# A banded attention and expert-routing kernel: the values become the held operand, in four 32-column strips, and the transposed probabilities stream past them

## The chip, the cores and the metric

The kernel runs on one core of a Trainium2 chip. The metric is device time in microseconds (us); three runs of the kernel before gave 1156.02 us as their median. Six engines matter: TensorE (PE in the profile, with its weight loads shown as PEld), VectorE (DVE), ScalarE (ACT), GpSimd (POOL), SyncE (SP) and the DMA queues. Each engine works through its own instructions in program order, and they meet at semaphores.

A matrix product here is always "held operand" against "streamed operand": the held one (128 partitions by up to 128 columns) is loaded into the array, the streamed one passes through it, and each held column becomes one partition of the result in PSUM.

## The reference

Eight sequences of 1024 tokens, 128 features, float32. The block is layer norm, windowed attention, residual, layer norm, a mixture of experts, residual:

```
q, k, v = split_heads(xn @ Wq), split_heads(xn @ Wk), split_heads(xn @ Wv)   # 16 heads of 8
scores  = einsum('bhld,bhlwd->bhlw', q, k_win) * scale      # each token sees the last 64 keys
attn    = softmax(scores)
ctx     = einsum('bhlw,bhlwd->bhld', attn, v_win)
x       = x + ctx @ Wo
...
expert_weights, top_experts = top_k(softmax(xf @ w_router), 2)   # 8 experts, capacity 2048 slots each
h = gelu(einsum('ech,ehf->ecf', xb, w1)); y = einsum('ecf,efh->ech', h, w2)
x = x + (gated y, added back to its tokens) + bias
```

## The kernel before

**Tiles and stages.** The 8192 tokens are 64 tiles of 128, worked in 32 pairs. The first stage (to about 800 us of the trace) does the attention of all pairs and, once per sequence of four pairs, the routing. The second stage (from about 846 us) runs the experts over gathered slots. The change touches the first stage.

**One pair.** A pair `n` has two tiles (`s` = 0, 1), each tile two blocks of 64 queries, each block 16 heads. The heads are worked in 8 slots per pair (`k` = 0 to 7): slot k belongs to tile k // 4, block (k // 2) % 2 and half of the heads k % 2, and holds four products `c` of two heads each. A row block of one product is 2 heads x 64 queries = 128, its columns are 128 keys, of which a window mask in `kT` leaves 64 per query.

**One slot on TensorE** (function `pair` of the tensor block, L1066):

- `probs_T(n, k)`, L1002: four transposes of the probabilities of this slot into the one PSUM bank `pt_ps`;
- `score(.., k + LEAD)`, L993: four score products, three slots ahead, into one of four banks;
- `weighted(.., k - 1)`, L1015: four products of the slot before. The held operand is the transposed probabilities (128 columns), the streamed one is the values of two heads and a column of ones (17 columns). The results lie as query rows in `o_ps[s]`, one bank per tile; the 17th column is the softmax's denominator;
- in some slots one of the small steps: `prep_T`, `query_key`, `values` for the next pair (L968 to L979), `context_T` (L1021) and `project` (L1029) of a finished tile, `router_T` and `router` (L1036, L1041).

Every float32 product is carried out as two instructions, each with its own weight load, so that four products stand as x8 in the trace; a transpose is one instruction.

**The other engines in a slot.** VectorE: `score_max` (L661) takes the row maximum of the scores, `probs_T` (L666) copies the transposed probabilities to SBUF in six of eight slots, layer-norm steps (L618 to L652) lie between; `normalise` (L673, L677) divides a finished tile's sums, `residual` (L685) adds the projected tile to `x_sb`. ScalarE: `exps` (L509, four activations, 128x128 each) three slots ahead, `probs_T` (L515) in slots 0 and 5, and copies for the small steps (L467 to L525). GpSimd: `spread_queries` (L360) builds the block-diagonal queries, and in the pair behind a routed one it issues the indirect DMAs that send rows to their slots (L370).

**What sets the order.** It is written out by hand: each engine has a function `pair` with the eight slots. A finished tile goes weighted -> normalise -> context_T (TensorE) -> context_T (ScalarE) -> project -> residual. TensorE waits before the first `weighted` of a tile until the residual of the last tile in that bank is done (`s_x2`), before `weighted` and before the next `probs_T` until the copy of the transposed probabilities is done (`s_pt_sb`).

Of the kernel before, what the change touches and what calls it, by code (L numbers as in the profile page):

```python
# [30 lines left out]
VW = 2 * DH + 2  # L31
# [16 lines left out]
def moe_block_kernel(nc, x, wq, wk, wv, wo, w_router, w1, w2, bias, out):  # L48
    ctx = ExitStack()
    with ctx:  # L50
# [51 lines left out]
        probs = sb("probs", [P, 4, 4, P])  # L102
        probsT = sb("probsT", [P, 2, 4, P])
        rden = sb("rden", [P, 2, 2 * HP])
        ctx_sb = sb("ctx_sb", [P, 2, 3 * HP, DH])
# [21 lines left out]
        w1_hl = sb("w1_hl", [P, 2, 2, F], F32R)  # L127
        xT_hl = sb("xT_hl", [P, 2, 2, 4 * P], F32R)
# [11 lines left out]
        o_ps = bank[5:7]  # L140
# [6 lines left out]
        def ctx_view(s):  # L147
            return o_ps[s][:, 0:2 * HP * VW].rearrange("p (j c) -> p j c", c=VW)

# [25 lines left out]
        s_pv = sem("s_pv")  # L175
        s_ctx = sem("s_ctx")
# [271 lines left out]
        def _(act):  # L448
# [67 lines left out]

            def context_T(n, s):
# [13 lines left out]
            def pair(n, g=None, first=False):  # L531
                for k in range(UNITS):
# [32 lines left out]
            walk(act, pair)  # L565
            context_T(NPAIR - 1, 1)
# [24 lines left out]
        def _(dve):  # L591
# [77 lines left out]
            def normalise(chain, n, s):  # L669

                dve.wait_ge(s_pv, UNITS * n + 4 * s + 4)
# [136 lines left out]
            for i, free in enumerate((s_x2, s_xn2T, s_lg_sb, s_pt_sb, s_rows, s_out, s_sent, f_added)):  # L808
                nc.vector.memset(scratch[:, i:i + 1], 0.0).then_inc(free, START)
# [40 lines left out]
            def pair(n, g=None, first=False):  # L850
                chain = Chain(n * PER + PRE + ROUTE_STEPS * pair.routed + (1 if first else 0))
                for k in range(UNITS):
# [14 lines left out]
                    if k == 0 and not first:  # L867
                        normalise(chain, n - 1, 1)
# [55 lines left out]
            def gated(ee, q, c):  # L924
# [6 lines left out]
                else:  # L931
# [3 lines left out]
                                        in0=o_ps[c % 2][:, :].rearrange("p (k d) -> p k d", k=4),  # L935
# [26 lines left out]
        def _(pe):  # L962
# [42 lines left out]
            def weighted(n, k):  # L1005
# [60 lines left out]
            def pair(n, g=None, first=False):  # L1066
                for k in range(UNITS):
# [5 lines left out]
                    if k > 0:  # L1073
                        weighted(n, k - 1)
                    elif not first:
                        weighted(n - 1, UNITS - 1)
# [3 lines left out]
                    if k == 1:  # L1080
                        if not first:
                            context_T(n - 1, 1)
                        query_key(n + 1)
                    if k == 2 and not first:
                        project(n - 1, 1)
                    if k == 3:
# [110 lines left out]
```

## Time and profile before

| | us |
|---|---|
| median of three runs | 1156.02 |
| lowest, highest | 1154.77, 1157.13 |
| span of the profiled execution | 1155.7 |
| TensorE busy, its weight loads busy | 990.6 (86%), 942.3 (82%) |
| VectorE busy | 644.9 (56%) |
| ScalarE busy | 609.6 (53%) |
| GpSimd busy | 488.5 (42%) |

The page gives the profiled execution by its span, 1155.7 us, which lies 0.3 us from the median of the runs; nothing else of that execution is timed. The span has to be read by stage. Until about 800 us it is a train of pairs, most of them 21.53 us long; in the expert stage other limits hold. Within a pair, the chain of waits and the order in time say which engine is the bound. A matmul's recorded duration includes the way through the array; what one costs in a row of many is the distance between the starts, so a group "x8" of length 0.89 us in the chain is eight at 0.112 us.

### The profile page before, as it was taken

The numbers are of one execution on the slowest core, as the hardware profiler recorded it, in microseconds if no ns is written. First come the engines' busy times: TensorE is split into PE (matmuls) and PEld (weight loads), VectorE is DVE, ScalarE is ACT, GpSimd is POOL, SyncE is SP. The second block draws the span as 40 slices with busy tenths as digits, with TensorE's granted clock in tenths as the row PEclk, the third lists the DMA queues.
The fourth block names the chain that finished last, engine by engine and source line by source line (L and its number), as shares of the span: only waits on it lengthen the run. The fifth ranks groups of instructions, "written<-read, shape, count | busy, mean of one in ns | idle before, by whom it ended". The sixth has DMA issues, their size and how long they took to land.

```text
span 1155.7 us, 24887 instructions
## 1 busy us (share of the span) xinstructions
PE 990.6 (86%) x7670; PEld 942.3 (82%) x7670; DVE 644.9 (56%) x1980; ACT 609.6 (53%) x1898; POOL 488.5 (42%) x445
## 2 busy tenths in 40 slices
PE   2999998899899889989997998999605998889791
PEld 1899998799799889988997997999604997878691
DVE  5777787488468747856774786578521121212110
ACT  2777676466467647655673765567202442434330
POOL 4122124421712352162135225212531877777777
PEclk9999999799799979988997998899656999889896
DMA  8900001100100110010011001000122455455533
GB/s 186 390 17 18 11 10 47 32 18 18 56 12 9 41 37 9 18 60 17 9 36 42 9 18 56 22 9 31 50 65 87 54 90 90 76 84 89 89 33 34
DMA packets 61821, 60.14 MB, mean 52 GB/s; under 512 B 6721, under 2 KB 50648, under 8 KB 60736
## 3 DMA queue, kind: packets, MB, share of 16 engines
q1 hardware_dynamic: 34944, 40.18, 10.6%
q0 software_dynamic: 22528, 17.22, 10.3%
q10 hardware_dynamic: 4288, 2.10, 1.2%
q8 instruction: 18, 0.29, 0.1%
q14 instruction: 43, 0.35, 0.1%
HBM read 17.70 MB, written 31.59 MB: 43 GB/s over the span
## 4 chain that ended last, share of the span: by engine, by line
PE 44%; issue 18%; POOL 11%; DVE 11%; another core or an unknown queue 6%; ACT 4%; DMA 3%; ACTq 1%; DVEq 1%; POOLq 0%; SPq 0%
PE bank L993 15%; PE bank L1015 11%; POOL out L429 11%; PE bank L1002 8%; PE bank L1029 2%; DMA out<-y_sb,xg 2%; ACT probs L509 2%; ACT kT L479 2%; DVE negmax L661 2%; DVE probsT L666 1%; PE bank L979 1%; PE bank L1021 1%; DVE xn L652 1%; PE bank L973 1%
## 5 line engine op out<-in xcount | busy, mean ns | idle before, releaser
L509 ACT ACTIVATE probs<-bank,negmax 128x128 f32<-128x128 f32 x1036 | 295.2, 368 | 285.2 <-DVE negmax L661 278.4
L360 POOL TENSOR_TENSOR qbd<-qT,quadmask 128x512 f32<-128x512 f32 x132 | 134.5, 1040 | 522.8 <-ACT qT L467 400.3
L993 PE MATMUL bank<-kT,qbd 128*128 (+1 forms) x2072 | 295.1, 289 | 0.0
L993 PEld LDWEIGHTS bank<-kT,qbd 128*128 128x128 f32 x2072 | 273.2, 206 | 0.0
L1015 PEld LDWEIGHTS bank<-v_sb,probsT 128*128 128x128 f32 x2048 | 263.1, 200 | 3.7 <-issue 3.4
L1015 PE MATMUL bank<-v_sb,probsT 128*128 (+1 forms) x2048 | 258.9, 259 | 3.7 <-issue 3.5
L429 POOL DMA_INDIRECT out<-y_sb,xg x128 | 198.2, 1548 | 81.0 <-DVE y_sb L934 42.0
L661 DVE TENSOR_REDUCE negmax<-bank 128x4 f32<-128x512 f32 x259 | 177.9, 687 | 75.5 <-PE bank L993 42.4
L1002 PE MATMUL bank<-ident,probs 128*128 128x128 f32 x1024 | 170.1, 291 | 39.2 <-ACT probsT L515 26.6
L666 DVE COPY probsT<-bank 128x512 f32<-128x512 f32 x192 | 132.5, 690 | 122.7 <-PE bank L1002 76.0
L1002 PEld LDWEIGHTS bank<-ident,probs 128*128 128x128 f32 x1024 | 125.0, 152 | 56.5 <-ACT probsT L515 30.6
L581 ACT ACTIVATE hT<-bank 128x512 f32<-128x512 f32 x128 | 76.5, 597 | 144.2 <-PE bank L1137 136.4
L370 POOL DMA_INDIRECT slots_dram<-send_rows,slot_id x112 | 109.1, 974 | 32.1 <-issue 32.1
L1147 PE MATMUL bank<-w_sb,hT 128*128 128x128 f32 x1024 | 121.9, 278 | 0.0
L1137 PE MATMUL bank<-xT_hl,w_hl 128*128 128x512 f32 x384 | 105.1, 426 | 17.9 <-DVE xT_hl L921 17.9
L1147 PEld LDWEIGHTS bank<-w_sb,hT 128*128 128x128 f32 x1024 | 119.5, 195 | 0.1
L1137 PEld LDWEIGHTS bank<-xT_hl,w_hl 128*128 128x128 f32 x384 | 75.6, 204 | 34.8 <-issue 11.1
L934 DVE TENSOR_TENSOR y_sb<-bank,xg 128x512 f32<-128x512 f32 x32 | 22.1, 691 | 124.9 <-DMA out<-y_sb,xg 67.3
L921 DVE TENSOR_TENSOR xT_hl<-bank,xT_hl 128x512 fp32r<-128x512 f32 x32 | 22.1, 690 | 113.6 <-ACT xT_hl L574 102.8
L479 ACT COPY kT<-bank 32x256 f32 (+1 forms) x264 | 83.2, 361 | 2.4
L1124 PE MATMUL bank<-ident,xg 128*128 128x128 f32 x128 | 21.0, 290 | 34.5 <-DMA xg<-slots_dram 34.5
L1124 PEld LDWEIGHTS bank<-ident,xg 128*128 128x128 f32 x128 | 17.1, 151 | 39.6 <-issue 31.0
(114 smaller groups left out, 930.6 us busy)
## 6 DMA issues: line engine op xcount, KB each, us to landing
slots_dram<-empty_rows SPq DMA_DIRECT2D x8, 1096.0 KB, 15.4
xg<-slots_dram SPq DMA_DIRECT2D x32, 274.0 KB, 4.3
rows_sb<-xn SPq DMA_DIRECT2D x33, 128.0 KB
out<-xbias SPq DMA_DIRECT2D x32, 128.0 KB
w_sb<-in_L_ffn_w SPq DMA_DIRECT2D x16, 256.0 KB
send_rows<-rows_sb SPq DMA_DIRECT2D x7, 548.0 KB, 3.0
out<-y_sb,xg POOLq DMA_INDIRECT x128
slots_dram<-send_rows,slot_id POOLq DMA_INDIRECT x112
```

What stands on the lines that cost most here:

```text
L360: last = pool.tensor_tensor(out=qbd[s][half][:, :, :, :], in0=q.unsqueeze(2).to_broadcast([P, 2, HQ, BLK]), in1=heads.to_broadcast([P, 2, ...
L370: pool.indirect_dma_start(out=slots_dram, out_offset=bass.IndirectOffsetOnAxis(ap=slot_id[:, k, j:j + 1].bitcast(U32), axis=0), in_=rows[: ...
L429: pool.indirect_dma_start(out=out, out_offset=bass.IndirectOffsetOnAxis(ap=xg[:, r, 4 * c + k, ROW - 1:ROW].bitcast(U32), axis=0), in_=y_s ...
L479: last = nc.scalar.copy(windows.rearrange("p (t w) j -> p t w j", t=2), blocks[:, :, odd, :].unsqueeze(2).to_broadcast([32, 2, 2, BLK]))
L509: last = nc.scalar.activation(probs[:, k % 4, c, :], scores[k % 4][:, c * P:(c + 1) * P], ACT.Exp, bias=negmax[:, k % 4, c:c + 1])
L661: nc.vector.tensor_reduce(negmax[:, k % 4, :], scores[k % 4][:, :].rearrange("p (c j) -> p c j", c=4), AX.X, ALU.max, negate=True).then_in ...
L666: nc.vector.tensor_copy(probsT[:, k % 2, :, :].rearrange("p c j -> p (c j)"), pt_ps[:, :]).then_inc(s_pt_sb, 1)
L993: last = mm(scores[k % 4][:, c * P:(c + 1) * P], qbd[s][half][:, blk, h:h + 2, :].rearrange("p h q -> p (h q)"), keys.rearrange("p o j -> ...
L1002: last = nc.tensor.transpose(pt_ps[:, c * P:(c + 1) * P], probs[:, k % 4, c, :], ident[:, :])
L1015: last = mm(ctx_view(s)[:, blk * HP + j, 0:2 * DH + 1], probsT[:, k % 2, c, :], v, start=True, stop=True)
L1137: last = mm(bank[f][:, :], w1_hl[:, r, a, f * P:(f + 1) * P], xT_hl[:, c % 2, b, :], start=(i == 0), stop=(i == 2))
L1147: last = mm(o_ps[c % 2][:, k * D:(k + 1) * D], hT[:, c % 2, f, k * P:(k + 1) * P], w2_sb[:, r, f, :], start=(f == 0), stop=(f == FC - 1))
```

## The change

It turns the weighted sums round. The values of two heads, with their ones column, become the held operand: `VW` grows from 18 to 32, so that a product's values fill a strip of 32 columns, and the four products of a slot use the four strips of the array, with their results in partitions 0-31, 32-63, 64-95 and 96-127 of one new bank `u_ps`. The transposed probabilities, 128 columns, stream. The sums of a tile then lie transposed (values by queries). For every tile ScalarE copies the whole bank to SBUF (`weighted_out`, a new 128x512 copy), and TensorE transposes it back by four transposes (`weighted_T`) into `o_ps`, where `normalise` finds it as before, at a distance of 32 instead of 18.

There is one bank `u_ps` and one bank `o_ps` now for both tiles. The first `weighted` of a tile waits until `weighted_out` of the tile before has run (`s_u_sb`); `weighted_T` waits for that copy and for the residual of the tile before (`s_x2`); `normalise` waits for `weighted_T` (`s_uT`). The steps of the second tile move by one slot: `normalise` on VectorE from slot 0 to 1, `context_T` from slot 1 to 2 on TensorE and ScalarE, `project` from slot 2 to 3. TensorE's loop is written out over the four pairs of a sequence. `probs` gets another place in SBUF, and the expert stage addresses the same two banks by other names.

```diff
-VW = 2 * DH + 2
+VW = 32
...
-        o_ps = bank[5:7]
+        u_ps = bank[5]
+        o_ps = [bank[6], bank[6]]
...
+            def weighted_out(n, s):
+                act.wait_ge(s_pv, UNITS * n + 4 * s + 4)
+                nc.scalar.copy(u_sb[:, s, :, :].rearrange("p i q -> p (i q)"), u_ps[:, :]).then_inc(s_u_sb, 1)
...
-                    if k == 1 and not first:
+                    if k == 0:
+                        if not first:
+                            weighted_out(n - 1, 1)
+                        prep_T(n + 1)
+                    if k == 2 and not first:
                         context_T(n - 1, 1)
-                    if k == 0:
-                        prep_T(n + 1)
+                    if k == 4:
+                        weighted_out(n, 0)
...
-                dve.wait_ge(s_pv, UNITS * n + 4 * s + 4)
+                dve.wait_ge(s_uT, 2 * n + s + 1)
...
-                    if k == 0 and not first:
+                    if k == 1 and not first:
                         normalise(chain, n - 1, 1)
...
                 if k % 4 == 0:
-                    pe.wait_ge(s_x2, START + 2 * n - 1 + s)
+                    pe.wait_ge(s_u_sb, START + 2 * n + s)
                 for c in range(4):
-                    j = 4 * half + c
-                    v = v_sb[:, bass.ds(n % 2, 1), 2 * s + blk, j, 0:2 * DH + 1].rearrange("p o c -> p (o c)")
-                    last = mm(ctx_view(s)[:, blk * HP + j, 0:2 * DH + 1], probsT[:, k % 2, c, :], v, start=True, stop=True)
+                    v = v_sb[:, p % 2, 2 * s + blk, 4 * half + c, :]
+                    last = mm(u_ps[32 * c:32 * c + 32, (k % 4) * P:(k % 4 + 1) * P], v, probsT[:, k % 2, c, :],
+                              start=True, stop=True)
                 last.then_inc(s_pv, 1)
+
+            def weighted_T(n, s):
+                pe.wait_ge(s_u_sb, START + 2 * n + s + 1)
+                pe.wait_ge(s_x2, START + 2 * n + s)
+                for i in range(4):
+                    last = nc.tensor.transpose(o_ps[s][:, i * P:(i + 1) * P], u_sb[:, s, i, :], ident[:, :])
+                last.then_inc(s_uT, 1)
```

On TensorE, in slots 5 and 6 of a pair, this stands before (L1002 is `probs_T`, L993 `score`, L1015 `weighted` of the slot before, L1036 `router_T`, L1021 `context_T`):

```order
L1002 MATMUL bank<-ident,probs 128x128 [waits s_pt_sb,s_exp]
L1002 MATMUL bank<-ident,probs 128x128 x3
L993 MATMUL bank<-kT,qbd 128x128 [waits s_k_sb,s_qbd]
L993 MATMUL bank<-kT,qbd 128x128 x3
L1015 MATMUL bank<-v_sb,probsT 128x17 [waits s_x2,s_pt_sb]
L1015 MATMUL bank<-v_sb,probsT 128x17 x3
L1036 MATMUL bank<-ident,xn 128x128 [waits s_xn2,s_v_sb]
```

and in the same place this stands now (L1016 `probs_T`, L1007 `score`, L1029 `weighted`, L1037 `weighted_T`, L1058 `router_T`):

```order
L1016 MATMUL bank<-ident,probs 128x128 [waits s_pt_sb,s_exp]
L1016 MATMUL bank<-ident,probs 128x128 x3
L1007 MATMUL bank<-kT,qbd 128x128 [waits s_k_sb,s_qbd]
L1007 MATMUL bank<-kT,qbd 128x128 x3
L1029 MATMUL bank<-probsT,v_sb 32x128 [waits s_u_sb,s_pt_sb]
L1029 MATMUL bank<-probsT,v_sb 32x128 x3
L1037 MATMUL bank<-ident,u_sb 128x128 [waits s_x2,s_u_sb]
L1037 MATMUL bank<-ident,u_sb 128x128 x3
L1058 MATMUL bank<-ident,xn 128x128 [waits s_xn2,s_v_sb]
```

The first product of the tile's second half of slots now waits for ScalarE's copy instead of for a residual, and four transposes follow it.

On ScalarE, slots 4 to 6 of a pair stand so before (L509 `exps`, L515 the copy of the transposed probabilities, L525 `router_T`):

```order
L509 ACTIVATE probs<-bank,negmax 128x128 x4
L515 COPY probsT<-bank 128x512
L507 ISA
L509 ACTIVATE probs<-bank,negmax 128x128 x4
L524 REGISTER_ALU
L525 ACTIVATE xn2T<-bank 128x256
```

and so now (L514 `exps`, L524 `weighted_out`, L520 the copy of the transposed probabilities, L534 `router_T`):

```order
L514 ACTIVATE probs<-bank,negmax 128x128 x4
L524 COPY u_sb<-bank 128x512
L520 COPY probsT<-bank 128x512
L512 ISA
L514 ACTIVATE probs<-bank,negmax 128x128 x4
L533 REGISTER_ALU
L534 ACTIVATE xn2T<-bank 128x256
```

The new copy stands behind the slot's four exponentials and ahead of the copy that TensorE's next transposes wait for.

## Rows read from the trace of the kernel before

**Rows 1.** Page: busy time of each engine, and TensorE's granted clock in 40 slices.

```profile
PE 990.6 (86%) x7670; PEld 942.3 (82%) x7670; DVE 644.9 (56%) x1980; ACT 609.6 (53%) x1898; POOL 488.5 (42%) x445
...
PEclk9999999799799979988997998899656999889896
```

**Rows 2.** Busy time by stretch: three whole pairs of 21.53 us apart, a routed pair, two behind it.

```profile
core 0: us, PE busy (x) PEld busy (x) DVE busy (x) ACT busy (x) POOL busy (x), PEclk, DMA share, GB/s
240.80:262.33 21.53, 21.53 (x189) 21.08 (x188) 16.28 (x49) 15.61 (x55) 4.76 (x5) 1.00 0.04 12
...
571.93:595.15 23.22, 22.36 (x199) 21.51 (x199) 21.38 (x76) 15.87 (x54) 4.76 (x5) 1.00 0.04 12
595.15:627.70 32.55, 27.15 (x190) 26.09 (x190) 15.96 (x48) 14.39 (x49) 20.33 (x21) 0.84 0.18 60
627.70:652.85 25.15, 23.49 (x189) 22.66 (x190) 17.08 (x53) 16.99 (x58) 4.76 (x5) 0.93 0.04 11
```

**Rows 3.** Chain of waits over one pair (240.8 to 262.4): start, length, what.

```profile
241.48 0.89 PE bank L993 x8
242.37 0.80 PE bank L1015 x8
...
256.86 0.44 PE bank L1002 x4
```

**Rows 4.** TensorE in time, 246.2 to 251.0: start, length; across a 64-row group.

```profile
247.86 0.96 PE L1015 MATMUL bank<-v_sb,probsT 128*128 x8
248.76 0.71 PE L1029 MATMUL bank<-wo_sb,ctxT 64*128 64x128 f32 x4
249.40 0.66 PE L1002 MATMUL bank<-ident,probs 128*128 128x128 f32 x4
249.89 1.06 PE L993 MATMUL bank<-kT,qbd 128*128 x8
```

**Rows 5.** TensorE in time, 252.0 to 259.2: slots 4 and 5.

```profile
252.12 0.60 PE L1002 MATMUL bank<-ident,probs 128*128 128x128 f32 x4
...
253.45 0.96 PE L1015 MATMUL bank<-v_sb,probsT 128*128 x8
...
254.74 1.06 PE L993 MATMUL bank<-kT,qbd 128*128 x8
255.63 0.96 PE L1015 MATMUL bank<-v_sb,probsT 128*128 x8
```

**Rows 6.** VectorE in the same stretch.

```profile
252.81 0.68 DVE L666 COPY probsT<-bank 128x512 f32<-128x512 f32 x1
253.41 0.86 DVE L618 BATCH_NORM_STATS2 stats<-x_sb 128x6 f32 x4
254.19 0.68 DVE L661 TENSOR_REDUCE negmax<-bank 128x4 f32<-128x512 f32 x1
```

**Rows 7.** ScalarE in the same stretch.

```profile
254.90 1.14 ACT L509 ACTIVATE probs<-bank,negmax 128x128 f32<-128x128 f32 x4 [0.81 <-DVE negmax L661]
255.91 0.60 ACT L515 COPY probsT<-bank 128x512 f32<-128x512 f32 x1
```

**Rows 8.** ScalarE, then TensorE, in slots 0 and 1 (240.8 to 245).

```profile
243.13 1.14 ACT L509 ACTIVATE probs<-bank,negmax 128x128 f32<-128x128 f32 x4 [1.03 <-DVE negmax L661]
244.15 0.39 ACT L486 COPY xnT<-bank 128x256 f32<-128x256 f32 x1
...
244.60 0.63 PE L1015 MATMUL bank<-v_sb,probsT 128*128 x5
```

**Rows 9.** Longest waits of 595 to 653, the two pairs behind a routed one.

```profile
ACT probs L509 <- DVE negmax L661: 25.7, 13, 7.6
...
DVE probsT L666 <- remote: 7.1, 2, 4.1
```

**Rows 10.** Page: GpSimd's issues to the slots (busy, mean ns).

```profile
L370 POOL DMA_INDIRECT slots_dram<-send_rows,slot_id x112 | 109.1, 974 | 32.1 <-issue 32.1
```

More of the change, by code:

```diff
@@ L127, in moe_block_kernel @@
         w1_hl = sb("w1_hl", [P, 2, 2, F], F32R)
+        with nc.sbuf_tensor("probs", [P, 4, 4, P], F32) as probs:
+            pass
         xT_hl = sb("xT_hl", [P, 2, 2, 4 * P], F32R)
@@ L565, in _ @@
             walk(act, pair)
+            weighted_out(NPAIR - 1, 1)
             context_T(NPAIR - 1, 1)
@@ L806, in _ @@
             nc.vector.memset(kT[96:128, 3, 0, :], 0.0)
-            for i, free in enumerate((s_x2, s_xn2T, s_lg_sb, s_pt_sb, s_rows, s_out, s_sent, f_added)):
+            for i, free in enumerate((s_x2, s_xn2T, s_lg_sb, s_pt_sb, s_u_sb, s_rows, s_out, s_sent, f_added)):
                 nc.vector.memset(scratch[:, i:i + 1], 0.0).then_inc(free, START)
@@ L1003, in probs_T, with weighted @@
                 last.then_inc(s_pt, 1)
-            def weighted(n, k):
+            def weighted(n, p, k):
                 s, blk, half = k // 4, (k // 2) % 2, k % 2
@@ L1064, in counts, with pair @@
                 last.then_inc(s_pos, 1)
-            def pair(n, g=None, first=False):
+            def pair(n, p, g=None, first=False):
                 for k in range(UNITS):
@@ L1073, in pair @@
                     if k > 0:
-                        weighted(n, k - 1)
+                        weighted(n, p, k - 1)
                     elif not first:
-                        weighted(n - 1, UNITS - 1)
+                        weighted(n - 1, p + 1, UNITS - 1)
                     if k == 0:
@@ L1081, in pair @@
                         if not first:
-                            context_T(n - 1, 1)
+                            weighted_T(n - 1, 1)
                         query_key(n + 1)
                     if k == 2 and not first:
-                        project(n - 1, 1)
+                        context_T(n - 1, 1)
                     if k == 3:
+                        if not first:
+                            project(n - 1, 1)
                         values(n + 1)
                     if k == 5:
+                        weighted_T(n, 0)
                         pe.wait_ge(s_v_sb, n + 2)
@@ L1098, in pair @@
                         project(n, 0)
-            pair(0, first=True)
+            pair(0, 0, first=True)
             pe.wait_ge(c_pool, 21)
-            walk(pe, pair)
-            weighted(NPAIR - 1, UNITS - 1)
+            for p in range(1, PAIRS_PER_SEQ):
+                pair(p, p)
+            with pe.Fori(1, BATCH) as b:
+                for p in range(PAIRS_PER_SEQ):
+                    pair(b * PAIRS_PER_SEQ + p, p, b - 1 if p == ROUTED_AT else None)
+            weighted(NPAIR - 1, PAIRS_PER_SEQ - 1, UNITS - 1)
+            weighted_T(NPAIR - 1, 1)
             context_T(NPAIR - 1, 1)
@@ L1146, in results @@
                     for f in range(FC):
-                        last = mm(o_ps[c % 2][:, k * D:(k + 1) * D], hT[:, c % 2, f, k * P:(k + 1) * P],
+                        last = mm(bank[5 + c % 2][:, k * D:(k + 1) * D], hT[:, c % 2, f, k * P:(k + 1) * P],
                                   w2_sb[:, r, f, :], start=(f == 0), stop=(f == FC - 1))
```

8 lines of the change are left out of this document (5 added, 3 removed).

## The prediction, made before the changed kernel had run

> **What bounds the kernel now.** I read the page first [rows 1]: TensorE is busy for 86% of the span, no other engine for more than 56%, and its clock, in tenths, stands at 9 in most slices with dips to 7. That is a mean over stages, so I cut the stretch of pairs into its pairs. The common pair takes 21.53 us, and TensorE is busy in all 21.53 of it, at full clock, with VectorE at 16.28, ScalarE at 15.61 and GpSimd at 4.76 [rows 2]. The routed pair takes 23.22 (TensorE 22.36, VectorE 21.38). The pair behind it takes 32.55, with 5.4 us in which TensorE is idle and a clock of 0.84; the one after that 25.15. There ScalarE waits for VectorE's maxima, VectorE waits for something that the profile calls remote [rows 9], and GpSimd is busy for 20.33 us with its issues at 0.97 us each [rows 2, 10]. So four pairs take 102.4 us, and 25 of 32 pairs go at TensorE's pace or nearly so; seven do not. The expert stage is untouched.
>
> Then the chain of waits over a common pair: it never leaves TensorE. Eight score instructions take 0.89 us, 0.112 each; the weighted sums go at the same pitch (0.80, and the rest stands in the next piece); four transposes take 0.44, 0.109 each [rows 3]. The weighted sums stream 17 columns and the scores 128, yet both need 0.112 us an instruction. The sums thus pay for loading 128 held columns, and the scores for streaming 128, or for both.
>
> **The products turned round.** 8 slots of 8 instructions a pair, 0.89 us each slot. The held operand shrinks to 32 columns, the streamed one grows from 17 to 128, so one instruction alone still costs about 0.112 us: nothing is won but by strips that run side by side. The trace has no strips, so I bound a slot's products. Above: one instruction after the other, 8 x 0.112 = 0.89 us. Below: all four strips at once and only the two instructions of one product behind each other, 2 x 0.112 = 0.22. In every row instructions start in program order, and the two of one product stand next to each other and use the same strip. The second must wait for the first, and the next product's first can start only behind that second. So the eight overlap only at the three joints between products: 5 x 0.112 = 0.56 us. I take that, which is worked out from the scores' pitch, and keep both ends for the range.
>
> **Changing the shape of the array.** `project` is the one group now that uses the array in another shape, 64*128. From the start of the weighted group ahead of it to the next score group are 249.89 - 247.86 = 2.03 us [rows 4]; where nothing stands between, 254.74 - 253.45 = 1.29 [rows 5]. The difference of 0.74 is 4 x 0.112 = 0.45 for its instructions and 0.29 for going into the shape and out again. I take 0.30 for both, 0.15 for one. Every slot would now go in and out: 8 x 0.30 a pair. The bounds are nothing (only a cut by rows pays) and 0.30. `project` stands right behind the strips in slots 3 and 7, so that one of its own changes goes: -0.15 x 2.
> The Trainium skill says in "TensorEngine Tiling (Array Packing)", Key Properties, that a change of tiling mode, and not only of the tile, drains the engine. The trace shows it for 64 rows; no row shows it for 32 columns. By that rule the price of 0.30 would hold for the strips too, and it speaks against this change.
>
> So a slot's group costs 0.56 + 0.30 = 0.86 against 0.89: -0.03, or -0.3 us a pair. TensorE's main gain is eaten by the shape changes.
>
> **The way back.** Eight transposes a pair at 0.109: +0.9 us, all on TensorE, which has no gap. Sum on TensorE: -0.3 - 0.3 + 0.9 = +0.3.
>
> **The new copy.** ScalarE gets two 128x512 copies a pair, 0.60 each [rows 7]: 15.6 + 1.2 = 16.8 of 21.5, which fits. But TensorE now waits for them, since there is one bank `u_ps`. In slot 5 the first sums of tile 1 need `weighted_out` of tile 0. What is queued ahead of that copy on ScalarE is four exponentials, which need VectorE's maximum of scores that TensorE made in slot 4. Before, the four transposes of slot 4 end at 252.72; VectorE copies (252.81), takes the layer norm's statistics (253.41, 0.86), the maximum (254.19) [rows 5, 6]; the exponentials start at 254.90, and the next copy at 255.91 lasts until 256.51 [rows 7]. The new copy takes that place. With 0.1 for the signal, the sums can load at 256.6; now they load 0.11 before their start at 255.63, at 255.52 [rows 5]. Stall: 1.1 us. What was next on ScalarE, the copy of the transposed probabilities, comes 0.6 later, at 257.1, while TensorE's transposes that need it stand behind the late sums (0.86) and the four new transposes (0.44): covered. In slot 0 the exponentials end at 244.15 (the next copy's start), the new copy at 244.75, so the sums can load at 244.85 in place of 244.49 [rows 8]: 0.35 us. Below, these stalls could be nothing if ScalarE ran further ahead; it does not, it waited 0.81 and 1.03 us for the maxima there. If TensorE became faster per slot by some amount, each stall would grow by that amount: the path over VectorE and ScalarE does not shrink. VectorE's division now waits for the way back, but its result is needed one slot later and it has over 5 us a pair to spare. Sum of stalls: 1.45.
>
> **The sum.** A pair at TensorE's pace: +0.3 + 1.45 = +1.75 us; 25 of them, +44. In the seven long pairs 5.4 us of idle TensorE hide the transposes; the copy (0.6 each) stands in their chain through ScalarE: I take +0.7, with 0 and 1.75 as bounds, so +5. At the end of the stage one copy and four transposes lengthen the last tile: +1, and the longer fill of ones in `v_sb` at the start under +1. 1155.7 (the span) + 44 + 5 + 2 = 1207. The span is 0.3 us below the median of the runs, so that I name 1207 for the run as well. Its own range is 1190 to 1225.
>
> **The rivals.**
> *Strips one after another* (22%). A slot's products take 0.89 + 0.30: +0.30 x 8 = +2.4, with -0.3 and +0.9; the stalls shrink to 0.8, since TensorE comes later itself. +3.8 x 25 = +95, the long pairs +10, the ends +2: 1263. For it: two float32 instructions with 32-column loads between, and no row shows two matmuls side by side. Against it: held weights and PSUM partitions are disjoint.
> *Strips overlap fully, or the shape change is free* (22%). With all four at once, 0.22 + 0.30 a slot: -0.37 x 8 = -3.0, -0.3 and +0.9 make -2.4, but the stalls grow by 0.34 each to 2.1: -0.3 x 25 = -7, +5 + 2: 1156. With no price for the shape but 0.56 for the products: -0.33 x 8 + 0.9 = -1.7, stalls 2.05: +0.35 x 25 = +9, +7: 1171. So even the gain that was worked out comes back as a wait for ScalarE. Together 1148 to 1176.
> The Trainium skill, "TensorE: Matmul & The Clock Gate", Measured speedup vs the span model, has packed products start about 4 ns apart and three column strips at 2.38 times the speed. That would put the four strips at the lower bound here, if the two instructions of a product did not stand between; no run here shows it yet.
> *Both* (10%): 0.22 us a slot, no shape price. -0.67 x 8 + 0.9 = -4.5; stalls 1.45 + 2 x 0.64 = 2.7; -1.8 x 25 = -45 + 7: 1118. ScalarE, with 16.8 us of work and waits of 0.8 to 1 us in several slots, would then be the bound, so 1118 to 1140.
> *The clock falls* (8%). TensorE has no idle time in a common pair now and a clock of 1.00; where it is idle for 5.4 of 32.55 us, the mean clock is 0.84 [rows 2]. With 1.45 us of stall and the shape changes in 23 us it could spend part of each pair at the lower of its two levels, 1.2 in place of 2.4 GHz. At a mean clock of 0.93, as in the pair of 25.15, some 7% of the pair is added to the forecast: 25 x 1.6 = +40: 1247. It decides once it touches the common pairs, not only the ones behind the routed one. Against it: the pair of 23.22 has 0.9 us of idle TensorE and still 1.00.
>
> **How the numbers follow.** Forecast 38%, strips in turn 22%, full overlap or free shape 22%, both 10%, clock 8%. Cases of both signs exist, but those on the slower side hold most of the chance. The range 1142 to 1268 holds the forecast, the clock case, the middle cases and somewhat over half of the strips in turn, which itself is uncertain by 15 us either way: about 82%. About 0.2% (2.3 us) is what a measurement of this kernel can tell from no change. Faster: the 10% of both and 9 of the 22% around 1156 and 1171, 20% in all with rounding; within 0.2%: 5%; slower: 75%.
>
> **What the profile of the changed kernel would show.** The chain of a common pair: still TensorE, now broken twice by ScalarE's copy `u_sb` and VectorE's maximum. TensorE in time: from the last score start to the next group's first start about 0.97 us if I am right, near 1.3 if the strips go in turn, near 0.64 if they overlap fully. Waits: TensorE's `weighted` line on ScalarE's `u_sb` copy, about 1.1 us and 0.35 us, once each a pair. A common pair of 23.3 us. The forecast is wrong if a common pair is under 22 or over 24.5 us, if no gap stands at the strips' edges, or if that wait is missing.

## The result: 1.5% slower, and the profile after

| | before | after |
|---|---|---|
| median of the runs, us | 1156.31 | 1174.04 |
| span of the profiled execution, us | 1155.7 | 1171.7 |
| stage of pairs (second pair's preparation to the last's) | 768.8 | 783.0 |

The ratio is 1.015, with a 95% interval of 1.0136 to 1.0165: 17.7 us slower. 1207 was forecast with a range of 1142 to 1268. The sign holds and the time lies in the range, but the loss is 17.7 us where 51 were forecast, a third. On a second chip, both kernels again gave 1157.8 and 1182.2 us (below), a ratio of 1.021.

First the page: busy time of each engine [rows 1].

```profile
PE 907.6 (77%) x7926; PEld 772.3 (66%) x7926; DVE 666.4 (57%) x1981; ACT 641.4 (55%) x1962; POOL 489.2 (42%) x445
```

TensorE has lost 83 us of busy time (990.6 before) and the kernel is slower. Then busy time by stretch [rows 2]: an early common pair, a later one, a routed one, the two behind it.

```profile
core 0: us, PE busy (x) PEld busy (x) DVE busy (x) ACT busy (x) POOL busy (x), PEclk, DMA share, GB/s
96.80:118.75 21.95, 19.72 (x200) 16.58 (x196) 16.71 (x50) 16.62 (x55) 4.82 (x5) 1.00 0.05 13
351.04:373.46 22.42, 19.75 (x200) 16.55 (x197) 17.39 (x50) 16.62 (x55) 4.76 (x5) 1.00 0.05 13
373.46:396.43 22.97, 20.14 (x209) 16.85 (x206) 20.47 (x74) 16.88 (x56) 4.76 (x5) 1.00 0.04 12
396.43:432.00 35.57, 22.74 (x196) 18.93 (x196) 18.95 (x50) 16.76 (x55) 20.40 (x21) 0.82 0.17 57
432.00:455.05 23.05, 20.13 (x201) 16.93 (x197) 17.74 (x51) 16.51 (x55) 4.76 (x5) 0.98 0.05 14
```

A common pair, 21.53 us before, is 21.95 early and 22.42 later, and TensorE now idles for some 2.7 us of it. The routed pair went from 23.2 to 23.0. The two behind it: before 57.7 together, now 58.6. Summed over the stage: the first six pairs +2.8, seven routed ones -1.9, six later common ones +5.3, the twelve behind routed ones +7.9 (the six with the sends +10.6, the six after them -2.6); the start -1.3 and what follows the last pair +3.1. That is the 16.0 us between the spans.

TensorE in time, slots 3 to 5 of the common pair (start, length) [rows 5]:

```profile
358.48 0.43 PE L1029 MATMUL bank<-probsT,v_sb 128*32 128x128 f32 x8
359.43 0.71 PE L1051 MATMUL bank<-wo_sb,ctxT 64*128 64x128 f32 x4 [0.53 <-ACT ctxT L528]
360.73 0.71 PE L993 MATMUL bank<-wv_sb,xnT 128*128 128x128 f32 x4 [0.59 <-ACT kT L484]
...
361.72 1.06 PE L1007 MATMUL bank<-kT,qbd 128*128 128x128 f32 x8
362.70 0.42 PE L1029 MATMUL bank<-probsT,v_sb 128*32 128x128 f32 x8
363.06 0.66 PE L1016 MATMUL bank<-ident,probs 128*128 128x128 f32 x4
363.55 1.06 PE L1007 MATMUL bank<-kT,qbd 128*128 128x128 f32 x8
365.69 0.42 PE L1029 MATMUL bank<-probsT,v_sb 128*32 128x128 f32 x8 [1.08 <-ACT u_sb L524]
366.04 0.66 PE L1037 MATMUL bank<-ident,u_sb 128*128 128x128 f32 x4
```

and the same slot 4 before [rows 5]:

```profile
252.56 1.06 PE L993 MATMUL bank<-kT,qbd 128*128 x8
253.45 0.96 PE L1015 MATMUL bank<-v_sb,probsT 128*128 x8
254.26 0.63 PE L1002 MATMUL bank<-ident,probs 128*128 128x128 f32 x4
254.74 1.06 PE L993 MATMUL bank<-kT,qbd 128*128 x8
```

The strips' eight instructions last 0.42 us with their way through the array, against 0.96. From score group to score group, slot 4 takes 363.55 - 361.72 = 1.83 us where it took 254.74 - 252.56 = 2.18. Three times in these rows TensorE waits for ScalarE: for the copied context (0.53), the keys (0.59) and the copied sums (1.08). ScalarE in the same stretch [rows 7]:

```profile
359.00 0.38 ACT L528 ACTIVATE ctxT<-bank 64x256 f32<-64x256 f32 x1
359.40 1.28 ACT L484 COPY kT<-bank 32x256 f32 x4
...
364.01 1.14 ACT L514 ACTIVATE probs<-bank,negmax 128x128 f32<-128x128 f32 x4 [0.93 <-DVE negmax L675]
365.03 0.60 ACT L524 COPY u_sb<-bank 128x512 f32<-128x512 f32 x1
365.50 0.62 ACT L520 COPY probsT<-bank 128x512 f32<-128x512 f32 x1
```

The chain of waits over that place shows the path of the prediction: maximum, exponentials, copy, sums.

```profile
363.39 0.60 DVE negmax L675
...
364.28 0.88 ACT probs L514 x3
365.16 0.48 ACT u_sb L524
365.64 0.04 issue
365.69 0.42 PE bank L1029 x8
```

Slot 1 has the same wait, shorter:

```profile
353.29 0.42 PE L1029 MATMUL bank<-probsT,v_sb 128*32 128x128 f32 x8 [0.47 <-ACT u_sb L524]
```

The figure in brackets is idle time of the array alone. Measured from start to start, less the 0.20 us that stands at an edge of the strips anyway, the waits of the common pair are 0.54 (slot 1), 0.60 for the context and 0.66 for the keys (slot 3), and 1.15 us (slot 5): 2.95 in all.

### The profile page after: what moved, and what is told of

Read it like the earlier page. It is cut to its first block, busy times and chain, and to the rows that moved or that the text cites. A ratio compares the mean times of both kernels' runs of the same rounds, so it can differ in the third digit from the quotient of the medians.

```text
span 1171.7 us, 24626 instructions
## 1 busy us (share of the span) xinstructions
PE 907.6 (77%) x7926; PEld 772.3 (66%) x7926; DVE 666.4 (57%) x1981; ACT 641.4 (55%) x1962; POOL 489.2 (42%) x445
## 3 DMA queue, kind: packets, MB, share of 16 engines
q8 instruction: 76, 1.25, 0.4%
## 4 chain that ended last, share of the span: by engine, by line
PE 29%; issue 21%; DVE 15%; ACT 13%; POOL 11%; another core or an unknown queue 5%; DMA 3%; ACTq 1%; DVEq 1%; POOLq 0%; SPq 0%
POOL out L434 10%; PE bank L1007 7%; ACT probs L514 7%; PE bank L1016 6%; DVE negmax L675 5%; PE bank L1029 4%; PE bank L1037 4%; ACT kT L484 3%; ACT u_sb L524 3%; DMA out<-y_sb,xg 2%; DVE stats L632 2%; PE bank L993 2%; PE bank L1051 1%; PE bank L987 1%
## 5 line engine op out<-in xcount | busy, mean ns | idle before, releaser
L514 ACT ACTIVATE probs<-bank,negmax 128x128 f32<-128x128 f32 x1036 | 296.6, 371 | 241.0 <-DVE negmax L675 228.3
L1007 PE MATMUL bank<-kT,qbd 128*128 128x128 f32 x2072 | 285.2, 283 | 0.0
L1007 PEld LDWEIGHTS bank<-kT,qbd 128*128 128x128 f32 x2072 | 264.1, 200 | 0.0
L1016 PE MATMUL bank<-ident,probs 128*128 128x128 f32 x1024 | 166.1, 287 | 22.4 <-DVE probsT L680 14.2
L1029 PE MATMUL bank<-probsT,v_sb 128*32 128x128 f32 x2048 | 113.2, 294 | 90.1 <-ACT u_sb L524 82.3
L1016 PEld LDWEIGHTS bank<-ident,probs 128*128 128x128 f32 x1024 | 124.7, 149 | 38.0 <-DVE probsT L680 17.1
L1029 PEld LDWEIGHTS bank<-probsT,v_sb 128*32 128x32 f32 x2048 | 42.2, 110 | 125.5 <-ACT u_sb L524 64.1
L1177 PE MATMUL bank<-w_sb,hT 128*128 128x128 f32 x1024 | 119.4, 275 | 0.0
L1177 PEld LDWEIGHTS bank<-w_sb,hT 128*128 128x128 f32 x1024 | 116.9, 192 | 0.1
L1051 PE MATMUL bank<-wo_sb,ctxT 64*128 64x128 f32 x256 | 45.9, 300 | 18.7 <-ACT ctxT L528 12.4
L1051 PEld LDWEIGHTS bank<-wo_sb,ctxT 64*128 64x128 f32 x256 | 33.5, 188 | 34.0 <-ACT ctxT L528 21.0
```

The lines of the kernel that those rows point to most:

```text
L514: last = nc.scalar.activation(probs[:, k % 4, c, :], scores[k % 4][:, c * P:(c + 1) * P], ACT.Exp, bias=negmax[:, k % 4, c:c + 1])
L1007: last = mm(scores[k % 4][:, c * P:(c + 1) * P], qbd[s][half][:, blk, h:h + 2, :].rearrange("p h q -> p (h q)"), keys.rearrange("p o j -> ...
L1016: last = nc.tensor.transpose(pt_ps[:, c * P:(c + 1) * P], probs[:, k % 4, c, :], ident[:, :])
L1029: last = mm(u_ps[32 * c:32 * c + 32, (k % 4) * P:(k % 4 + 1) * P], v, probsT[:, k % 2, c, :], start=True, stop=True)
L1177: last = mm(bank[5 + c % 2][:, k * D:(k + 1) * D], hT[:, c % 2, f, k * P:(k + 1) * P], w2_sb[:, r, f, :], start=(f == 0), stop=(f == FC - 1))
```

## The experiments

Two explanations stand against each other. Theory W: the strips give their full gain, and waits for ScalarE take it back. Rival P: shape changes and transposes eat the gain. Unless said otherwise an edit is made to the changed kernel; ratios are to the kernel before, run beside it.

### 1. Where ScalarE's copy stands, and the shared bank

First, on ScalarE, `weighted_out` ahead of the exponentials (its two calls behind them go):

```diff
                     if k in BY_ACT:
                         probs_T(n, k)
+                    if k == 0 and not first:
+                        weighted_out(n - 1, 1)
+                    if k == 4:
+                        weighted_out(n, 0)
                     if k + LEAD < UNITS:
                         exps(n, k + LEAD)
...
-                            weighted_out(n - 1, 1)
...
-                    if k == 4:
-                        weighted_out(n, 0)
```

> The changed kernel, but on ScalarE the copy of the sums stands ahead of the slot's four exponentials in slots 0 and 4 instead of behind them. Theory W (the strips pay in full, and waits for ScalarE's copy give it back): in the changed kernel's common pair TensorE's sums wait 0.5 us in slot 1 and 1.15 us in slot 5 for that copy; ahead of the exponentials it falls into ScalarE's wait for the maximum, so both waits go: -1.6 us in some 25 pairs, about 1134 us. Rival P (TensorE's changes of shape and the eight transposes eat the gain, and VectorE and ScalarE would set the pace anyway): the waits only move, 1165 to 1176 us.

1156.5 us, ratio 0.998 (0.997 to 1.000): between the two cases. Both waits for the copy are gone from the common pair, which takes 21.29 us: 1.13 less, not 1.6, since the router's logits now wait some 0.25 us and three smaller gaps of 0.08 us open; the slot-3 waits stay as they were. The six pairs with sends grew from 209 to 224 us, while the six after them fell by 15.

Then a bank of its own for each tile; `weighted_T` no longer waits for a residual, since `weighted` does:

```diff
-        u_ps = bank[5]
-        o_ps = [bank[6], bank[6]]
+        u_ps = o_ps = bank[5:7]
...
-                    pe.wait_ge(s_u_sb, START + 2 * n + s)
+                    pe.wait_ge(s_x2, START + 2 * n - 1 + s)
...
-                pe.wait_ge(s_x2, START + 2 * n + s)
```

> The changed kernel, but each tile's sums have a bank of their own and are transposed back into the same bank; the order on ScalarE stays. The sums of the next tile no longer wait for the copy, only the transposes behind them do. Theory W: of the 0.5 and 1.15 us of wait a pair 0.4 each is covered by the sums themselves: -1.0 us in 25 pairs, about 1148 us. Rival P: no change beyond 5 us, 1168 to 1176 us.

1152.5 us, 0.996 (0.994 to 0.997), nearer theory W. Common pair 21.60; of the waits for the copy, 0.78 us before `weighted_T` in slot 5 and 0.1 in slot 1 are left.

Both edits together:

> Both edits: the copy ahead of the exponentials, and a bank of its own for each tile. Theory W: the two take away the same waits, so hardly more than the copy's place alone: 1128 to 1136 us. Rival P: 1165 to 1176 us. If the remaining wait for ScalarE in slot 3 (0.5 us for context, 0.8 us for the keys) grows in their place, 1145 to 1155 us.

1143.5 us, 0.987 (0.986 to 0.989). That is in none of the three cases and nearest the last, but not for its reason: the slot-3 waits are 0.60 and 0.66 us, as before, and have not grown. The common pair is 21.29 as with the copy first alone; the gain over it lies in the pairs with sends (206 us for six in place of 224). Rival P falls: TensorE's instructions and their order are the same in these three, only what they wait for and where they write differs, and 17.6, 21.5 and 30.5 us of the 1174.0 came off.

### 2. What the strips do

One strip for all four products of a slot:

```diff
-                    last = mm(u_ps[32 * c:32 * c + 32, (k % 4) * P:(k % 4 + 1) * P], v, probsT[:, k % 2, c, :],
+                    last = mm(u_ps[0:32, (k % 4) * P:(k % 4 + 1) * P], v, probsT[:, k % 2, c, :],
```

> The changed kernel, but the four products of a slot all use the first strip of 32 columns and write the same 32 partitions, so that three of four heads' sums are lost (the other partitions of the bank hold ones). Shape changes, copy and transposes stay. Theory W: the eight instructions go one after another at 0.112 us, 0.89 us in place of 0.24: +5.2 us a pair on TensorE, of which the waits for ScalarE's copy give back up to 2: +3.2 to +4 us in 25 pairs, 1250 to 1275 us. If strips gave nothing, 1174 us.

1257.8 us, 1.086 (1.084 to 1.089), as theory W had it. The common pair is 25.06, 2.64 more. Read from the single records of the trace, the eight starts stand 0.109 us apart (the first two 0.133), 0.79 us in all, where four strips have them within 0.154: four starts 7 ns apart, and from 0.133 on four more.

```profile
386.15 1.06 PE L1008 MATMUL bank<-kT,qbd 128*128 128x128 f32 x8
387.13 1.06 PE L1030 MATMUL bank<-probsT,v_sb 128*32 128x128 f32 x8
388.13 0.66 PE L1038 MATMUL bank<-ident,u_sb 128*128 128x128 f32 x4
```

Two strips, products 0 and 1 on the first and 2 and 3 on the second:

```diff
-                    last = mm(u_ps[32 * c:32 * c + 32, (k % 4) * P:(k % 4 + 1) * P], v, probsT[:, k % 2, c, :],
+                    last = mm(u_ps[32 * (c // 2):32 * (c // 2) + 32, (k % 4) * P:(k % 4 + 1) * P], v, probsT[:, k % 2, c, :],
```

> The changed kernel, but products 0 and 1 of a slot use the first strip of 32 columns and products 2 and 3 the second, so half of the heads' sums are lost (the rest of the bank holds ones). It tells how four strips come to take two pitches and not the five of the prediction. From the first to the last recorded start of the eight instructions four strips took 0.15 us and one strip 0.79. Theory F (starts strictly in order, the two halves of a product next to each other, as the prediction had it): 6 pitches between, 0.65 us, about 1235 us. Theory I (in order, but the first halves of all four products stand before the second halves): 4 pitches between, 0.44 us, about 1205 us. Theory Q (each strip runs its own instructions, whatever stands between them): 3 pitches between, 0.33 us, about 1193 us.

The starts stand at 0, 13, 133, 146, 242, 255, 351 and 365 ns, within 4 ns in 220 of 256 groups: three pitches, theory Q. The records do not name the strip of a start, but the other two theories would need four and six pitches. So two strips run side by side although the kernel's order puts the first strip's four instructions ahead of the second's. The common pair is 23.25 us, between 22.42 and 25.06.

This kernel and e10 (below) ran where the kernel before took 1075.5 us, so their totals (1143.7 and 1120.3) compare only with that: 1.063 and 1.041. The waits that the profile calls remote, 67 us on VectorE in the first trace, are missing from both traces, and GpSimd issues its DMAs as before (0.97 us each); why is open. A later kernel on the same chip had them again.

### 3. Side edits, and the price of a shape alone

The kernel before with the change's side edits alone: TensorE's loop written out, `VW = 32` and the new place of `probs`.

> The kernel before with the change's side edits alone: TensorE's loop written out over four pairs, values at a distance of 32, probs at its new place; sums as before. Theory W: none of these is on the way of a pair that TensorE keeps busy: common pair 21.53 us, within 3 us of the kernel before. Rival S (the longer instruction stream or the new places cost part of the 17.7 us): 1160 us or more.

1158.0 us, 1.001 (1.000 to 1.002), common pair 21.53. Theory W.

The kernel before with its projection over all 128 rows:

```diff
-        wo_sb = sb("wo_sb", [HP * DH, 2, D])
+        wo_sb = sb("wo_sb", [P, 2, D])
...
-        ctxT = sb("ctxT", [HP * DH, 2, 2, 2, BLK])
+        ctxT = sb("ctxT", [P, 2, 2, 2, BLK])
```

> The kernel before, but the projection uses all 128 rows of the array (rows 64 to 127 of its weights are zero), so that the only group with another shape has the common one. It tells the price of a shape change by itself. Theory W: 0.30 us for going in and out, twice a pair: common pair 20.93 us, -15 us in 25 pairs, about 1141 us. Rival (the 0.29 us that was read lies in something else, the wait for the copied context or ScalarE's copy): within 3 us of the kernel before.

1154.1 us, 0.997 (0.996 to 0.998). The total is 2.6 us less, the rival's case, but its reason does not hold: the common pair lost 0.31 us of the 0.60. In the trace the stretch from the sums' start over the projection to the next score start is 0.25 us shorter (1.78 where it was 2.03 [rows 4]), but TensorE then waits 0.16 us for the keys in slot 3. So the price of going in and out is real, 0.25 rather than 0.30, and ScalarE's keys are near the bound already in the kernel before. Less arrives in the total because the twelve pairs behind routed ones took 2.9 us more than in the first trace; why is open.

### 4. The wait in slot 3

The context transposes of the second tile (TensorE) and their copy (ScalarE, shown) at the end of slot 1 instead of in slot 2:

```diff
                     if k == 1:
                         query_key(n + 1)
                         keys(n + 1, (0, 1))
+                        if not first:
+                            context_T(n - 1, 1)
...
-                    if k == 2 and not first:
-                        context_T(n - 1, 1)
```

> The changed kernel with one edit alone: the second tile's context transposes and their copy at the end of slot 1 instead of in slot 2. In the changed kernel's common pair TensorE waits 0.60 us for the copied context and 0.66 us for the keys in slot 3, which the prediction did not have. Theory W: half or more of these 1.26 us goes, 0.5 to 1.0 us in 25 pairs, 1149 to 1162 us. Rival: the two waits for the copied sums grow by as much, 1171 to 1176 us.

It ran beside the kernel before at 1075.5 us (above), so it was run again, with both kernels and the best version so far:

> The kernel before, unchanged, traced where the next three run. In the last two experiments it took 1075.5 us in place of 1156 and VectorE's waits that the profile calls remote (67 us in the first trace) were missing from the traces of both. If this chip is like the first ones: 1154 to 1158 us, common pair 21.53, the pair with the sends near 32.6. If it is like the last: about 1075 us, common pair again 21.53, the pair with the sends near 25.

> The changed kernel, unchanged. On a chip like the first: ratio 1.0136 to 1.0165 as before. On a chip like the last: the common pair costs the same +0.88 us, but the long pairs are no longer held by the sends and the change's cost shows there too, so 1120 to 1130 us, a ratio of 1.04 to 1.05.

> The changed kernel with the context early alone, beside the changed kernel itself on one chip. Theory W: the wait of slot 3 shrinks, common pair 22.17 against 22.42 us, 4 to 12 us less than the changed kernel. Rival: the same time within 2 us.

1157.8 us before, 1182.2 changed (1.021, 1.0195 to 1.0229), 1181.6 with the context early (1.020). The common pair fell from 22.42 to 22.16: the wait for the context (0.60) went, the keys' (0.68) stayed, 0.27 came in front of the context. The early pairs rose from 21.96 to 22.41. The rival holds by its time, though not by its reason: the waits for the copied sums did not grow (1.08 us of idle time in slot 5 before the edit, 1.07 with it). The six later common pairs gave 1.6 us, the early ones took 0.8 of it back, and the routed ones stayed as they were. The common pair of the changed kernel repeats to 0.01 us on both chips; the six pairs with sends do not (209 and 226 us). The stretch of one of them in the second trace of the changed kernel, then waits in it (total, times, longest):

```profile
291.74:330.32 38.58, 23.50 (x197) 19.52 (x197) 18.55 (x52) 16.75 (x55) 20.29 (x21) 0.80 0.16 53
```

```profile
PE bank L1029 <- ACT u_sb L524: 6.8, 2, 5.9
...
DVE probsT L680 <- remote: 5.5, 1, 5.5
...
PE bank L1051 <- ACT ctxT L528: 4.5, 2, 4.1
DVE negmax L675 <- remote: 4.3, 1, 4.3
```

While GpSimd sends, single VectorE instructions start 4 to 6 us late for something that the profile calls remote, and the wait for ScalarE's copy, 1.15 us in a common pair, becomes 5.9. That the sends are behind these waits is shown further down: without them VectorE has no remote wait in the whole trace.

On top of e3, the context early:

> The changed kernel with the copy first and own banks, and besides the second tile's context transposes and their copy stand at the end of slot 1 instead of in slot 2. In the common pair of the kernel without this (21.29 us) TensorE waits in slot 3, 0.5 us for the copied context and 0.6 us for the keys, with ScalarE idle from 344.14 to 344.72 just ahead. Theory W: 0.4 to 0.8 us less in 25 pairs, 1124 to 1134 us. Rival D (VectorE's maxima behind the layer norm steps set the pace in slots 1 to 5): the wait moves to slot 4, within 4 us of 1143.5.

1139.1 us, 0.983 (0.982 to 0.985), common pair 21.05: 0.24 less. The 4.4 us lie between the two cases. With the projection over all rows:

> The kernel with the copy first, own banks and the context early, with the projection over all 128 rows too. The projection follows the strips, so one shape change of two goes: 0.15 us twice a pair. Theory W, if TensorE is still the pace in those slots: 4 to 8 us less than with the context early alone. Rival D: no more than 2 us less.

1136.9 us, 0.982 (0.980 to 0.984): 2.3 us less, again between the cases, and by the totals not told from the one before; the common pair fell to 20.92. Repeated beside the kernel before of the second chip:

> The best version so far (copy first, own banks, context early, full rows), unchanged. On a chip like the first 1134 to 1139 us, ratio 0.982. On a chip like the last its common pair is 20.92 against 21.53 as there; 1065 to 1090 us, and whether it still beats the kernel before depends on its long pairs.

1134.0 us, 0.980 (0.978 to 0.981).

Then the keys, ahead of the exponentials in slot 2:

```diff
+                    if k == 2:
+                        keys(n + 1, (2, 3))
                     if k + LEAD < UNITS:
                         exps(n, k + LEAD)
...
-                    if k == 2:
-                        keys(n + 1, (2, 3))
```

> The best version so far (copy first, own banks, context early, full rows) with one more edit: in slot 2 ScalarE copies the second half of the keys ahead of the four exponentials. In its common pair of 20.92 us TensorE's value products wait 0.68 us for these keys. Theory W: that wait goes, 0.4 to 0.7 us in 25 pairs, 1116 to 1128 us. Rival D (the exponentials, 0.6 us later, are then late for VectorE and TensorE): within 3 us of the best version or slower, 1131 to 1140 us.

**1118.3 us, 0.967 (0.965 to 0.968): the best version, 39 us faster than the kernel before beside it.** Common pair 20.04. The wait for the keys, which the prediction did not have, is gone, and 0.9 us a pair with it: in the trace without this edit it was 0.76 us from start to start, and some 0.16 less now stand before the router's logits. A stretch of 20.20 us among the common pairs, in which TensorE is idle for 0.20:

```profile
335.10:355.30 20.20, 20.00 (x200) 16.51 (x199) 18.04 (x58) 16.60 (x56) 4.77 (x5) 1.00 0.05 14
```

### 5. The sends, and a long branch

The kernel before without the DMAs that send rows to their slots:

```diff
-                        pool.indirect_dma_start(
...
+                        pool.sem_inc(s_scat, 16)
```

> The kernel before without GpSimd's 128 indirect DMAs that send rows to their slots (the semaphore is counted up instead; the experts then work on empty slots). It takes the cause out of the long pairs. Theory L (the sends alone make the pair behind a routed one 32.6 us and the one after it 25.1): both fall to near 21.5 us, and the stage of pairs to about 690 us. If another cause holds them long: above 25 us.

1046.0 us. The pair with the sends falls from 32.6 to 21.53, exactly a common one; the one after it is 23.5. The stage of pairs takes 693.4 us, and VectorE has no remote wait left (67 us in the first trace). Theory L holds for the kernel before, except for 2 us in the pair after. Another 36 us went behind the pairs, where the experts work on empty slots.

The changed kernel without them:

> The changed kernel without the sends, beside the one before without them. Theory L: without sends every pair is common or routed, and the change costs what the common pairs cost: 7 x (-0.27) and 24 x 0.5 to 0.9, +12 to +20 us in the stage of pairs, with the long pairs' further +9 to +16 us gone. Rival: the long pairs keep a share of the loss without the sends, over +25 us.

1081.6 us, so 35.6 more, and the rival holds: the pair behind a routed one keeps some 27.0 us. Six such pairs hold 32 of the 36 us. Near the end of one:

```profile
207.34 0.71 PE L1047 MATMUL bank<-wo_sb,ctxT 64*128 64x128 f32 x4
211.06 0.65 PE L1012 MATMUL bank<-ident,probs 128*128 128x128 f32 x4 [3.02 <-issue]
```

TensorE idles for 3 us for nothing that the profile shows. Then its granted clock falls to the lower level, 1.2 GHz, for 3.4 us from 212.3 on; behind the later five branches it does so for 6.8 us each. In the trace its branch back to the loop's start lasts 3.3 to 4.2 us in every kernel with strips and four pairs written out, and 0.21 in the kernel before and in e5, whose loop is written out too. The pages' instruction queue (packets, MB, share):

```profile
q8 instruction: 22, 0.36, 0.1%
```

for e5, and for the changed kernel

```profile
q8 instruction: 76, 1.25, 0.4%
```

Between two such branches e5 has some 1600 TensorE instructions in the trace, the changed kernel 1680. A body of two pairs, run twice:

```diff
-                for p in range(PAIRS_PER_SEQ):
-                    pair(b * PAIRS_PER_SEQ + p, p, b - 1 if p == ROUTED_AT else None)
+                with pe.Fori(0, 2) as i:
+                    for p in range(2):
+                        pair(b * PAIRS_PER_SEQ + i * 2 + p, p, b + i - 2 if p == 0 else None)
```

> The changed kernel, but TensorE's loop over the sequences has a body of two pairs run twice instead of four pairs written out; the small routing products of a routed pair are also issued, unused, in the first half (9 of them, about 0.3 us each sequence). In the traces of all kernels with the strips the branch back at the end of TensorE's body takes 3.3 to 4.0 us, and TensorE stands idle for 2.7 to 3.7 us there; in the kernel before, also with its loop written out (e5), the same branch takes 0.21 us. Theory C (the body with the strips' and transposes' extra instructions has become too long to stay loaded, and is fetched again at each branch): branches at 0.21 us, the q8 instruction traffic back from 1.25 MB to 0.3 to 0.5 MB, and 3.5 to 5.5 us less in six or seven long pairs: 20 to 38 us less than 1174 to 1182, about 1145 to 1160 us, so level with the kernel before. Rival H (in the full kernel the fetch hides behind the sends, as other waits do there): branches at 0.21 us all the same, but 1168 to 1182 us.

1180.5 us, 1.021 (1.019 to 1.022). All branches take 0.08 to 0.24 us and the queue moved 0.31 MB: with half the body the long branch is gone. The time is that of the changed kernel on the second chip (1182.2), not 20 to 38 us less: rival H. With the sends in place the long branch thus costs nothing that these runs can tell; the changed kernel itself varies by 8 us between chips. That it is the loss of the kernel without sends is read from the trace above (the idle time and the lower clock stand right behind it) and was not tested: the short body was not run without the sends.

## Why the prediction was right in sign and wrong in size

- **The bound**, right: TensorE set a common pair; taking work from it alone made it idle.
- **The products turned round**: the failed step. It had it that "the two of one product stand next to each other and use the same strip", so that the eight overlap "only at the three joints between products", 5 pitches, 0.56 us. Two strips show that every strip works through its own instructions, and four need two pitches: the lower bound, 0.22 us, that the prediction gave to a rival. From the last score start to the next group's start it named 0.97 us if it was right and 0.64 for full overlap; measured are 0.56 (0.205 + 0.153 + 0.203), where 0.925 stood before. A slot became 0.35 us shorter, not 0.03: some 2.5 us a pair were missed. The trace agrees in the main with what the prediction cites from the Trainium skill, "TensorE: Matmul & The Clock Gate", Measured speedup vs the span model, for packed products, starts about 4 ns apart: measured here are 7 ns, and the measurement decides.
- **The old price of the sums** was read a little too high: 8 x 0.112 = 0.89 us, but the group takes 254.26 - 253.45 = 0.81.
- **The shape change**: 0.30 forecast, 0.25 measured for rows by themselves. From the last score start to the strips 0.205 us pass, and from their last start to the next group 0.203, where 0.112 stood each time. That strips pay at both edges, as the 64-row group does, is shown; what TensorE does in that time is not.
- **The way back**: eight transposes, +0.9, as forecast (four stand 0.49 us from start to next start).
- **The new copy**: the mechanism and its places were right, 1.1 forecast and 1.15 measured in slot 5, 0.35 and 0.54 in slot 1. Moving the copy took both away.
- **Missed**: the waits in slot 3, 1.26 us a pair. I counted ScalarE's work by the pair (16.8 of 21.5, "which fits") and not by the slot; `context_T` was moved into the slot whose keys TensorE needs next. The trace before could have warned: in the routed pair TensorE already waits 0.46 us for the keys in slot 3.
- **The common pair** then sums to 21.53 - 8 x 0.35 - 0.1 x 2 (projection behind strips) + 0.9 + 2.95 = 22.4, as measured. Two errors, -2.5 and +1.3, with 0.3 of smaller ones left +0.88 of the forecast +1.75.
- **The sign was in good part luck.** With full overlap in its own sum the prediction gets 1156, no change. What makes a common pair slower beyond that are the slot-3 waits, which it did not have: 0.88 - 1.26 is below nothing. Of its own signs only the 0.56 us above speaks against it; a common pair of 22.42 lies above 22, and the edge gaps and the copy's waits are there.
- **25 pairs at +1.75**, +44 us forecast, are +3.6 measured. Six early ones have +2.8, six later common ones +5.3. The seven routed ones have -1.9: before, TensorE was idle there for 0.46 us before the keys and 0.41 before `probs_T`, so it was not the bound all along and the new waits fall in part on old ones. The six after the sends have -2.6.
- **The pairs with sends**: +0.7 each was too low, 10.6 us over six in the first trace. With the pairs after them that is +7.9, and +16.3 in the second. The changed chain puts one more VectorE-ScalarE hand-over behind instructions that start late while the sends run. Why the same kernel spreads so is open; the copy's place alone does not settle it, since moving it made these six longer still (224 us).
- **Rivals.** "Strips overlap fully" had the right mechanism and 1156; its range together with its neighbour, 1148 to 1176, holds the result, but not for its reason. It said that the stalls would grow by 0.34 each, but those two grew by 0.05 and 0.19 only, and the slot-3 waits came on top. "Strips one after another", 1263, is near what one strip costs: 1257.8. The granted clock of common pairs stayed at 1.00.

## What to carry to other kernels

When an operation that holds the bounding engine is made much shorter, list for each slot, not for each period, what the other engines have to deliver into it. Here three moves of ScalarE's copies (one with its transposes on TensorE), a bank for each tile and a projection over all rows turned +1.5% into -3.3% with the same products. Give a result that another engine must first empty its own bank, or the copy a place in front of work that waits for something else. And look at the branch of a loop that was written out: here it grew from 0.21 to over 3 us when the body grew by a twentieth, though another wait hides it today.

## What the runs showed of the hardware

- Eight float32 instructions with 32 held and 128 streamed columns start within 0.154 us on four strips, 0.365 on two and 0.79 on one. The starts on two strips fit only if each strip keeps just its own order.
- A group on strips, or on 64 rows, pays at its edges: 0.19 to 0.20 us from start to start where 0.112 stands between groups of one shape; 0.25 us for a 64-row group and back.
- TensorE's branch back took 0.21 us with a body of some 1600 traced instructions or fewer and 3.3 to 4.2 us with some 1680, with 1.25 MB instead of 0.36 MB through the instruction queue.
- VectorE's remote waits, 67 us in the first trace, are gone when GpSimd's sends are taken out, in both kernels.
- The kernel before had medians of 1156 to 1158 us on six occasions and of 1075.5 on one; the two kernels traced on that one have no remote waits on VectorE, though GpSimd sends.
